# Moving one of four one-hot tiles from VectorE to GpSimd, and reading row numbers one group ahead, in the second key's extra-row walk of a graph kernel

## The reference, cut to what matters

```
ex1 = e * x[src];  ex2 = e * x[dst]
mi = zeros.at[dst].add(ex1)
mo = zeros.at[src].add(ex2)
h = tanh(concat([mi, mo, x]) @ W1 + b1) ...
```

## Time and profile before

| what | value |
|---|---|
| median of 3 runs | 1683.98 us (1680.54 to 1688.54) |
| the profiled execution: its time | 1679.48 us |
| its span, first to last instruction | 1677.5 us |
| busy: PE / DVE / POOL / ACT | 1287.4 / 1219.6 / 1007.6 / 837.2 us |
| TensorE's mean granted clock | 0.855 of full speed |

### The profile page before, as it was taken

One profiled execution on the slowest core, in us unless ns is written; L12 is line 12 of the kernel. 1 busy time (PEld: TensorE's weight loads), 2 busy tenths in 40 slices (PEclk: granted clock), 3 DMA queues, 4 the chain that ended last, 5 costly groups with the idle time before them and its releaser, 6 DMA issues.

```text
span 1677.5 us, 26088 instructions
## 1 busy us (share of the span) xinstructions
PE 1287.4 (77%) x6396; PEld 930.4 (55%) x6396; DVE 1219.6 (73%) x3753; ACT 837.2 (50%) x2256; POOL 1007.6 (60%) x1084
## 2 busy tenths in 40 slices
PE   5699994686413777665677999975999999995773
PEld 1388883243212555555565666653777777775663
DVE  9699996677622343576667999983888888883776
ACT  0167771011101222566675777763665666554984
POOL 7777778777777777776111344446888666600444
PEclk8699997586755999988888999996999999997655
DMA  1100001223224889666455566631232223213785
GB/s 39 23 14 14 15 14 23 51 68 77 69 66 120 250 244 252 173 173 172 119 136 137 172 181 190 184 106 45 61 75 63 59 59 70 65 40 84 204 216 154
DMA packets 310023, 179.32 MB, mean 107 GB/s; under 512 B 29294, under 2 KB 303346, under 8 KB 309874
## 3 DMA queue, kind: packets, MB, share of 16 engines
q1 hardware_dynamic: 231234, 116.84, 26.7%
q0 software_dynamic: 29008, 36.18, 8.6%
q10 hardware_dynamic: 49632, 24.65, 5.1%
HBM read 111.48 MB, written 66.07 MB: 106 GB/s over the span
## 4 chain that ended last, share of the span: by engine, by line
PE 39%; POOL 25%; issue 15%; DMA 10%; DVE 6%; DVEq 2%; ACT 2%; SPq 1%; POOLq 0%; ACTq 0%
PE bank L1042 13%; POOL gat L536 12%; PE bank L1008 7%; POOL lined L544 7%; DMA lined<-in_x,other_i 5%; DVE res L1351 4%; PE bank L1035 3%; DMA placed<-pay,pos_i 3%; PE bank L959 3%; PE bank L1051 3%; POOL out L603 3%; PE bank L1001 3%; PE bank L1017 3%; PE bank L961 2%; POOL placed L555 2%
## 5 line engine op out<-in xcount | busy, mean ns | idle before, releaser
L593 POOL DMA_INDIRECT gat<-x_d,src_i x196 | 238.2, 1215 | 94.8 <-issue 55.7
L1351 DVE TENSOR_TENSOR res<-res,bank 128x128 f32 x588 | 168.5, 287 | 107.2 <-issue 22.6
L536 POOL DMA_INDIRECT gat<-in_x,key_i x196 | 207.0, 1056 | 61.9 <-issue 55.5
L555 POOL DMA_INDIRECT placed<-pay,pos_i x196 | 191.6, 978 | 69.8 <-issue 53.9
L544 POOL DMA_INDIRECT lined<-in_x,other_i x196 | 196.1, 1000 | 59.9 <-issue 48.6
L1042 PE MATMUL bank<-prod,ident 128*128 128x280 f32 x896 | 219.8, 404 | 0.0
L1042 PEld LDWEIGHTS bank<-prod,ident 128*128 128x128 f32 x896 | 168.7, 191 | 54.1 <-issue 15.2
L970 PE MATMUL bank<-woh,pw 128*128 128x128 f32 x784 | 133.4, 332 | 71.4 <-DVE woh L1330 35.8
L970 PEld LDWEIGHTS bank<-woh,pw 128*128 128x128 f32 x784 | 118.5, 235 | 86.7 <-DVE woh L1330 46.2
L56 ACT ACTIVATE xt<-bank 128x128 f32<-128x128 f32 x98 | 26.6, 271 | 264.8 <-PE bank L910 256.2
L890 PE MATMUL bank<-tile_oh,sel 128*128 128x196 f32 x784 | 142.6, 336 | 2.9 <-ACT tile_oh L663 2.0
(11 more groups left out here) (221 smaller groups left out, 2886.2 us busy)
## 6 DMA issues: line engine op xcount, KB each, us to landing
pw<-placed SPq DMA_DIRECT2D x588, 68.0 KB, 2.1
pw<-placed SPq DMA_DIRECT2D x98, 272.0 KB
xin<-in_x_t SPq DMA_DIRECT2D x53, 256.0 KB
placed<-pay SPq DMA_DIRECT2D x49, 272.0 KB, 2.4
x_d<-res POOLq DMA_DIRECT2D x49, 256.0 KB, 3.8
placed<-pay SPq DMA_DIRECT2D x28, 448.0 KB, 3.2
out<-out ACTq DMA_DIRECT2D x49, 256.0 KB, 2.7
xin<-in_x_t ACTq DMA_DIRECT2D x45, 256.0 KB
```

What stands on the lines that cost most here:

```text
L536: pool.indirect_dma_start(gat[:, t, :], None, x, bass.IndirectOffsetOnAxis(ap=key_i[:, 0, t:t + 1], axis=0)).then_inc(s_gat[t % G], 16)
L555: pool.indirect_dma_start(placed[1].rearrange("t p r -> (t p) r"), bass.IndirectOffsetOnAxis(ap=pos_i[:, 1, t:t + 1], axis=0), pay[i % 4][ ...
L593: pool.indirect_dma_start(gat1[g % 3][:, k, :], None, x1_d, bass.IndirectOffsetOnAxis(ap=src_i[:, t:t + 1], axis=0)).then_inc(c_gat[g % 3] ...
L1351: add.up(dve.tensor_tensor(into, into, quarter(bank + k // G, k % G), ALU.add))
```

## The change

In `D_EXTRA`, the first one-hot of each step is made by GpSimd, behind its two small instructions, with a signal `s_head` of its own, and TensorE waits for that in place of `s_woh`. VectorE has only the additions left there, and its register read for step `g + 1` now stands ahead of the additions of step `g`. In `D_FIRST`, whose one-hots VectorE still makes, TensorE's wait is renumbered, since `s_woh` now counts 49 fewer.

```diff
@@ gpsimd, loop over the second key's extra steps
                 pool.tensor_copy(rec[:, G * g:G * g + G, :], pw[i % 6][:, :, P:ROW]).then_inc(s_back, 1)
+                freed(pool, i - 3)
+                pool.tensor_scalar(woh[i % 4][:, 0, :], iota[:, 0:P], wxb[:, 1, G * g:G * g + 1], pw[i % 6][:, 0, P:P + 1],
+                                   ALU.add, ALU.is_equal).then_inc(s_head, 1)
@@ tensor, walk_extra and turn
-                pe.wait_ge(s_woh, i + 1)
+                if i < D_EXTRA:
+                    pe.wait_ge(s_woh, i + 1)
+                else:
+                    pe.wait_ge(s_head, i - D_EXTRA + 1)
...
-                pe.wait_ge(s_woh, i + 1)
+                pe.wait_ge(s_woh, D_EXTRA + b + 1)
@@ vector
-            def add_tiles(bank, t0, n, c):
+            def windows_at(t0, n, c):
                 _, to = nc.values_load_multi_w_load_instructions(
...
+                return to
+
+            def add_to(to, bank):
+                for k, w in enumerate(to):
+                    into = res[:, bass.ds(w, 1), :].rearrange("p o c -> p (o c)")
                     wait(dve, add.sem, add.n)
                     add.up(dve.tensor_tensor(into, into, quarter(bank + k // G, k % G), ALU.add))
+
+            def add_tiles(bank, t0, n, c):
+                add_to(windows_at(t0, n, c), bank)
...
-            staged([lambda g: hot_extra(D_EXTRA + g, 1), None, lambda g: add_extra(D_EXTRA + g, 1)], NG)
+            to = windows_at(0, G, 1)
+            for g in range(NG):
+                later = windows_at(G * g + G, G, 1) if g + 1 < NG else None
+                dve.wait_ge(s_wmm, D_EXTRA + g + 1)
+                add_to(to, WALK[(D_EXTRA + g) % 6])
+                to = later
```

More of the change, by code:

```diff
@@ L289, in gnn_kernel @@
         s_res, s_back, s_kr = sem("s_res"), sem("s_back"), sem("s_kr")
-        s_apart, s_away, s_hot = sem("s_apart"), sem("s_away"), sem("s_hot")
+        s_apart, s_away, s_hot, s_head = sem("s_apart"), sem("s_away"), sem("s_hot"), sem("s_head")
         s_ewt, s_ewt_sb, s_ewd = sem("s_ewt"), sem("s_ewt_sb"), sem("s_ewd")
@@ L1320, in _, with hot_extra @@
             payload(BOTH - 1)
-            def hot_extra(i, c):
+            def hot_extra(i):
                 g = i % NG
@@ L1326, in hot_extra @@
                 dve.wait_ge(s_pw[i % 6], pw_landed(i))
-                if c == 0:
-                    dve.tensor_tensor(kr[:, ts], wxb[:, c, ts], pw[i % 6][:, 1:G, P], ALU.subtract).then_inc(s_apart, 1)
+                dve.tensor_tensor(kr[:, ts], wxb[:, 0, ts], pw[i % 6][:, 1:G, P], ALU.subtract).then_inc(s_apart, 1)
                 freed(dve, i - 3)
-                dve.tensor_scalar(woh[i % 4][:, 0, :], iota[:, 0:P], wxb[:, c, G * g:G * g + 1], pw[i % 6][:, 0, P:P + 1],
+                dve.tensor_scalar(woh[i % 4][:, 0, :], iota[:, 0:P], wxb[:, 0, G * g:G * g + 1], pw[i % 6][:, 0, P:P + 1],
                                   ALU.add, ALU.is_equal).then_inc(s_woh, 1)
@@ L1347, in add_tiles @@
                     skip_runtime_bounds_check_because=IN_RANGE)
-                for k in range(n):
-                    into = res[:, bass.ds(to[k], 1), :].rearrange("p o c -> p (o c)")
+                return to
+            def add_to(to, bank):
+                for k, w in enumerate(to):
+                    into = res[:, bass.ds(w, 1), :].rearrange("p o c -> p (o c)")
                     wait(dve, add.sem, add.n)
                     add.up(dve.tensor_tensor(into, into, quarter(bank + k // G, k % G), ALU.add))
+            def add_tiles(bank, t0, n, c):
+                add_to(windows_at(t0, n, c), bank)
             def add_extra(i, c):
@@ L1363, in _ @@
                 for g in extra_steps(q):
-                    hot_extra(S_EXTRA + g, 0)
+                    hot_extra(S_EXTRA + g)
                 for g in extra_steps(q - 2):
```

## The result

The changed kernel took 1665.52 us (median of 4 runs, 1662.76 to 1667.35) against 1682.61 us (median of 4, 1680.54 to 1688.54) for the kernel before: a ratio of 0.9884, with a 95% interval of 0.9848 to 0.9919. Timed twice more, with 12 and 9 runs of it and 29 and 26 of the kernel before, it came to 0.9937 (0.9914 to 0.9959) and 0.9944 (0.9922 to 0.9966). So the change is faster, and by 9 to 11 us by the two larger measurements (with their intervals, 6 to 14); the 17 us (by the medians) to 20 us (by the ratio) of the first are 4 runs against 4, where the 29 and 26 executions of the kernel before in the larger ones lay 18 and 13 us apart.

The account below looks back on a forecast made before the run. The prediction took the walk to be bound by VectorE's serial chain, not throughput. Its terms, 11.0 + 2.3 - 0.5 = 12.8 us, took the median from 1683.98 to 1671.2 us, with an 8-in-10 range of 1664 to 1677.

Parts of the forecast that it names:

- Steps disturbed by TensorE: Second key's extra walk: steps where VectorE waited on late TensorE, 5.6 us, vanish as GpSimd makes the one-hot early.
- Start of the walk: Last first-key addition to first second-key addition: two reads in place of waiting, 0.93 us for 3.22, minus 2.3.
- The next stage's colder start: After the walk: TensorE, idle longer, gets going up to 3 us slower or not at all; 0.5 us taken.
- The read ahead: VectorE's register read for the next step, moved ahead of the additions: counted at no gain.
- 47 x 1.83 + 1.72 = 87.7: The walk's 48 step pitches without VectorE's compare: 87.7 us in place of 98.67, minus 11.0.
- The read hidden: Rival: VectorE's sequencer doesn't stop for the read, border 0.43 in place of 0.54 us; 5 us more, 1666; 17%.
- GpSimd's compare: GpSimd's one-hot in the walk: taken as 0.4 us, a GpSimd step of 0.81 us, hidden under the 1.83 us pitch.
- GpSimd's contention: Rival: GpSimd's compare holds up VectorE's additions through shared memory; 19.6 us added at full length, 1691; 6%.
- GpSimd as the bound: Rival: GpSimd's steps exceed 1.83 us; at a 2.5 us compare the walk ends 35 us later, 1719; 5%.
- Part given back: Rival: colder next stage or TensorE still late in some steps; 4 to 9 us less gain, 1675 to 1680; 9%.
- Nothing moves: Rival: another wait replaces the compare on VectorE; time stays within 4 us of 1684; 5%.
- The sum: Whole kernel: 11.0 + 2.3 - 0.5 = 12.8 us gained, from pitches, walk start and the next stage's colder start.

Follow-up runs that it names:

- hot_only: Changed kernel with each register read back behind its step's wait for TensorE; ratio 0.9906 to the kernel before, walk 91.24 us.
- dve_ahead: Kernel before with VectorE's compare three steps ahead of the additions in place of two; ratio 0.9969, walk 98.85 us.
- wait_on_add: Changed kernel, reads back behind TensorE's signal, second key's wait for the previous addition on the addition itself; ratio 0.9867 to the kernel before, walk 72.99 us.
- no_read: Changed kernel reading only the first step's numbers in the second key's extra walk, output wrong; ratio 0.972 to the kernel before, walk 67.18 us.
- read_mid: Changed kernel with the next step's read between the second and third addition; ratio 0.9889 to the kernel before, walk 93.54 us.
- pool_twice: Changed kernel with a second, unused GpSimd compare in each step; ratio 0.9971 to the kernel before, walk 94.08 us.
- beside_again: Kernel before with GpSimd also making a one-hot that nobody reads, timed on another chip than the first such run; ratio 0.9985.
- pool_beside: Kernel before with an added GpSimd compare per step into unused memory, on a chip taking about 1980 us; ratio 1.0015, walk 103.85 us.
- two_steps: GpSimd makes the one-hot; VectorE reads eight numbers every second step, behind the wait; ratio 0.9888 to the kernel before, walk 96.48 us.
- a_again: The changed kernel unaltered, second measurement against the kernel before; ratio 0.9937, walk 94.11 us.
- a_third: The changed kernel unaltered, third measurement against the kernel before; ratio 0.9944, walk 94.07 us.

## Why the prediction was right or wrong

**What held.** The bound was VectorE's serial chain, and taking the compare from it was worth about what the steps said. Steps disturbed by TensorE: all gone (the chain has no PE in it). Start of the walk: 3.22 to 0.96 us, minus 2.26, forecast minus 2.29. The two reads in it, the wait for the banks in place of the one-hot, the additions at 287 ns, the loads in time: as forecast. The next stage's colder start, for which I took 0.5 us and up to 3 as a bound, did not appear: the last step and the next matmul are 4.34 us apart (4.33 before), and the network's first layer, from that matmul to the end of GpSimd's last write of `x_d`, took 229.8 us after and 229.3 before.

**The step that failed** is "The read ahead. I count it at nothing", and with it "47 x 1.83 + 1.72 = 87.7". The 48 pitches took 91.57 us (795.25 to 886.82), 3.9 more than that. Three terms were missing. The wait for TensorE can no longer stand on the read, since the read is done earlier; it comes to the register instruction, which already waits for the addition before, and the second wait becomes an instruction of its own: 0.02 us and 0.05 to the next. The border is 0.59 in place of 0.54: 47 x 0.05 = 2.4 us. The last border, without a read, has the wait all the same, 0.50 in place of 0.43: 0.07 us. And four times in the walk an addition comes about 0.36 us late for nothing that the profile shows:

```profile
802.14 0.42 issue
...
826.45 0.06 DVEq L1359
826.50 0.40 issue
826.90 0.30 DVE res L1359
...
850.88 0.40 issue
...
875.24 0.40 issue
```

"Issue" is 0.40 or 0.42 where it is else 0.05, each time 24.4 us after the one before: 4 x 0.36 = 1.4 us. Counted in the traces, the distance is 128 of VectorE's instructions, those of its sequencer included. The changed kernel has 10 in a step, so 12.8 steps; `hot_only` has 9, and two of its four stand at 827.27 and 853.62 us, 26.4 apart, or 14.2 steps:

```profile
827.27 0.40 issue
...
853.62 0.40 issue
```

In all 16 traces that show two or more of them, the one of before among them, they are 128 or a multiple of it apart. In `wait_on_add` four steps take 1.61 to 1.82 us in place of 1.46 or 1.47, and in `no_read` none is late, so less of it reaches the additions where the sequencer runs ahead of them. What VectorE does there stays open. The forecast had put all that was above 93.1 us, 5.6 us, down to steps in which TensorE was late, and took it all away; `dve_ahead` has four late steps too, with TensorE out of the way. Together the three terms are 3.8 us, and they turn the 13.3 us that I forecast for the walk into the 9.4 measured. The order that I had read from the earlier trace rows was that of `hot_only`: its 48 pitches took 89.13 us, 1.4 over the forecast, which is its four late additions, and its walk fell by 12.2 us. The changed program had another order on one point: the row of the order itself, with two waits on one register instruction ("ISA [waits s_add,s_wmm]"), stands ahead of the prediction, and I passed over it.

**The read hidden** (17%, 5 us more) is refuted: most of its 0.34 us runs beside an addition, as it did before, but it holds what is behind it also with an addition between (`read_mid`), and also where the addition carries its own wait (`wait_on_add`: 0.50 us at the read, 0.32 elsewhere). The Trainium skill, "Advanced Engine Details and Errata", section Sequencer Loop, says that other engine instructions can be read and queued while a control instruction runs. No addition in these runs could show that: behind each read stands a register instruction first.

**GpSimd's compare** was mis-sized, 0.80 us where I took 0.4 (my own line between the two rows gave 0.46), twice the value taken and under the upper bound of 1.26. It cost nothing, since GpSimd's step (0.20 + 0.21 + 0.80 = 1.21 us) stayed under the pitch. Even twice the compare stayed hidden, at 1.87 us a step. The Trainium skill, "GPSIMD Engine Reference", section 4.1, has GpSimd near line rate for one input and about two times slower than VectorE for two. This compare has one tile as its input and took 2.4 times VectorE's 0.34 us; the measurement is above both, and it decides.

**GpSimd's contention** (6%) and **GpSimd as the bound** (5%) are refuted by `pool_twice`: 287 ns for the additions with GpSimd busy without a pause beside 169 of them, and the same walk, 94.08 us.

**Part given back** (9%, 4 to 9 us less gain) named the colder start and late steps of TensorE as its causes; neither came. The size came near it, by another way: 3.9 us less in the walk. **Nothing moves** (5%) is excluded by all three measurements.

**The sum** of 12.8 us against 9 to 11 in the two larger measurements: the walk gave 8.3 to 9.4, the shorter gathers may have given up to 4.3 more, of which the timed ratios of `beside_again` (minus 2.5 us, from minus 6.0 to plus 1.2) and `pool_beside` (plus 3.0, from minus 1.0 to plus 7.1) show nothing for sure. In the two profiled executions the 12.0 us are minus 9.4 in the walk, minus 5.4 up to its start, plus 2.7 after it; the part up to the start varies by 8.6 us between traces of kernels whose program is the same there (the placement's end at 787.56 to 796.13), so I read no more from it. What stays open is the surplus on one other chip: `two_steps`, `read_mid` and `no_read` were timed together and each gained 9 to 12 us more than its walk (18.8 against 7.0 us, 18.7 against 9.9, 47.1 against 36.3), with intervals of 6 to 10 us either way, while `dve_ahead`, timed beside them, gained 5.2 us with 4.6 in the walk. The three have GpSimd's compare and the short gathers, `dve_ahead` hasn't; but in the measurements with more executions a surplus of this size is not there (`a_again` 1.2 us, `a_third` none, `hot_only` 3.6). The median of 1665.52 came out 5.7 us below the 1671.2 predicted, but not because the walk gave more: it gave less. The first measurement's 17 to 20 us lie above the forecast gain and the later 9 to 11 below it, so that the forecast comes near the time is in part luck. The forecast also rests on a median of three runs that lay 5 to 7 us above the medians of the kernel before in the larger measurements (1676.78, 1679.16), which no row could have told.

## What to carry to other kernels

On an engine whose sequencer sets the pace, count the instructions on its queue between two engine instructions, and look where each wait lands. A wait that is moved onto an instruction that already waits becomes an instruction more, and one that stands on a register instruction keeps it from running beside the work before it: put it on the engine instruction itself. Work that sits in such a chain is worth moving to another engine even where it takes twice as long there, as long as that engine's step stays under the pitch.

## What the runs showed of the hardware

- A read of registers from on-chip memory takes VectorE's sequencer 0.34 us with four values and 0.60 with eight. Between additions that take 0.287 us, the read of four adds 0.09 to 0.11 us.
- A register instruction with a wait, ahead of an addition of 0.287 us, puts the additions 0.43 us apart; with the wait on the addition itself they are 0.32 apart. Against `hot_only`, with the same reads, the second form took 18 us from the walk (91.24 to 72.99), and in both keys' walks it gave the best kernel here, 0.9787 of the time before.
- A second wait on a register instruction became an instruction of its own and cost 0.07 us.
- GpSimd's compare of 128 columns with two per-partition operands takes 0.80 us, VectorE's 0.34. VectorE's additions of `res` and a PSUM bank stay at 287 ns beside it.
- On VectorE's queue something costs about 0.36 us every 128 instructions: once in 12.8 steps of the changed walk, once in 14.2 of `hot_only`.
- The shortest of GpSimd's gathers took 938 to 941 ns in all thirteen traces of kernels with a further GpSimd compare in a later stage, and 950 to 952 in all seven without it. What does it is open, and so is what it is worth.
- Two of the chips used took 1980 us for the kernel that takes 1680 on the others, with the same durations in the walk.
